# Bias addition and row minimum of a head in one VectorE instruction, early clears moved, the written-out orders redrawn

## The reference

```python
# block 1: 16 heads of 8 dims, relative-position bias, mask
energy = einsum('bhqd,bhkd->bhqk', Q, K) / sqrt(8) + bias[h, q, k]
energy = where(mask, neg, energy)
x = x + softmax(energy) @ V  (all heads) @ Wo + bo
# block 2: low-rank feed-forward with gelu, width 512
# block 3: the same attention without bias and mask
# block 4: 16 experts of width 64, each token's best 8, and a shared expert
```

## Time and profile before

| | us |
|---|---|
| median of 3 runs (lowest, highest) | 216.0 (214.54, 219.54) |
| the profiled execution | 216.93 |
| its span in the trace | 215.1 |
| PE busy in the span | 175.5 |
| DVE busy | 164.6 |
| ACT busy | 138.5 |
| POOL busy | 92.2 |

### The profile page before, as it was taken

How to read it: one execution, slowest core, us unless ns; L and a number is a source line. 1 busy time by engine, 2 the same in 40 slices (tenths; PEclk the granted TensorE clock), 3 DMA queues, 4 the chain that set the end, 5 groups by cost and what they waited for, 6 DMA issues and landing times.

```text
span 215.1 us, 4593 instructions
## 1 busy us (share of the span) xinstructions
PE 175.5 (82%) x1609; PEld 121.8 (57%) x1609; DVE 164.6 (76%) x459; ACT 138.5 (64%) x293; POOL 92.2 (43%) x109
## 2 busy tenths in 40 slices
PE   1550626999989789979759696999999999999994
PEld 0320413765556555756624493785676767788883
DVE  4269609969999999798897649599989597878643
ACT  2251404698889989999677948459389888233220
POOL 8186698699579969767123115110200011011000
PEclk9999955699999999999996978599999999999999
DMA  5352388214113650031200231200000100000000
GB/s 139 83 110 72 85 225 178 58 42 109 42 49 78 207 189 3 16 74 26 54 2 12 68 77 37 71 23 23 2 3 2 30 3 0 3 24 0 25 4 24
DMA packets 21879, 12.21 MB, mean 57 GB/s; under 512 B 3120, under 2 KB 21232, under 8 KB 21856
## 3 DMA queue, kind: packets, MB, share of 16 engines
q1 hardware_dynamic: 19776, 10.68, 19.6%
q10 hardware_dynamic: 2080, 1.24, 2.3%
HBM read 4.98 MB, written 0.54 MB: 26 GB/s over the span
## 4 chain that ended last, share of the span: by engine, by line
PE 55%; DVE 23%; ACT 5%; POOL 5%; issue 5%; SPq 2%; DMA 2%; ACTq 1%; DVEq 0%
PE bank L460 15%; PE bank L489 9%; PE bank L403 6%; PE bank L359 4%; PE bank L343 4%; DVE es L884 4%; PE bank L374 3%; DVE mx L893 3%; PE bank L439 2%; DVE q0p L1030 2%; SPq L211 2%; PE bank L476 2%; DVE x L934 2%; PE bank L429 2%; DVE ct L923 2%
## 5 line engine op out<-in xcount | busy, mean ns | idle before, releaser
L1766 POOL TENSOR_TENSOR es<-es,mx 128x512 f32<-128x512 f32 x32 | 33.6, 1065 | 8.0 <-DVE mx L889 7.8
L1744 POOL TENSOR_TENSOR rstd<-ve,half 128x2 f32<-128x2 f32 x16 | 11.1, 694 | 57.0 <-DVE ve L872 56.8
L1486 ACT ACTIVATE gth<-bank 128x256 f32<-128x256 f32 (+1 forms) x36 | 13.4, 382 | 24.6 <-PE bank L460 23.9
L403 PE MATMUL bank<-pt,va 128*32 128x128 f32 x512 | 27.3, 297 | 1.7 <-DVE es L884 0.6
L374 PE MATMUL bank<-ident,es 128*128 128x128 f32 x128 | 20.4, 291 | 4.6 <-ACT es L1426 2.9
L460 PE MATMUL bank<-xT,wg 128*128 128x256 f32 (+1 forms) x72 | 23.8, 414 | 0.0
L893 DVE TENSOR_REDUCE mx<-bank 128x4 f32<-128x512 f32 x32 | 20.5, 677 | 3.1 <-PE bank L359 3.1
L884 DVE TENSOR_TENSOR es<-bank,biasq 128x512 f32<-128x512 f32 x32 | 20.7, 679 | 2.1 <-PE bank L359 2.1
L460 PE MATMUL bank<-xT,wu 128*128 128x256 f32 (+1 forms) x72 | 21.9, 386 | 0.0
L489 PE MATMUL bank<-wd,hT 128*128 128x128 f32 x128 | 21.2, 289 | 0.0
L1426 ACT ACTIVATE es<-es 128x512 f32<-128x512 f32 x32 | 19.2, 624 | 2.8 <-POOL es L1766 2.8
(11 more groups left out here) (140 smaller groups left out, 359.4 us busy)
## 6 DMA issues: line engine op xcount, KB each, us to landing
k0st<-k0p SPq DMA_DIRECT2D x24, 64.0 KB, 2.0
k1st<-k1p SPq DMA_DIRECT2D x24, 64.0 KB, 2.0
q1st<-q1p SPq DMA_DIRECT2D x24, 64.0 KB, 2.0
q0st<-q0p SPq DMA_DIRECT2D x21, 64.0 KB, 2.0
biasq<-rel_bias_scratch SPq DMA_DIRECT2D x4, 256.0 KB, 5.2
wu<-in_wu SPq DMA_DIRECT2D x1, 544.0 KB, 3.9
wg<-in_wg SPq DMA_DIRECT2D x1, 544.0 KB, 4.9
x<-in_x SPq DMA_DIRECT2D x4, 128.0 KB, 3.7
```

What stands on the lines that cost most here:

```text
L403: ins = pe.matmul(dst[32 * s:32 * s + VW, h // 4 * SEQ:(h // 4 + 1) * SEQ], va[:, p, b, l, VCOLS * h:VCOLS * h + VW], pt[:, l, b, h], star ...
L1766: pool.tensor_tensor(es[:, b, h], es[:, b, h], mx[:, 0, p, b, h].unsqueeze(2).broadcast_to([128, 4, SEQ]), ALU.subtract).then_inc(nth(f"le ...
```

## The change

1. `add_bias` becomes four instructions, one per head of 128 columns. Each adds bias to scores and also writes the least of its row. `least` is gone, and `less_least` waits for the release of the chunk's bank, which the fourth instruction gives.
2. `first_queries_middle` makes the second bf16 part by a subtraction from the float32 values rather than by a cast of the remainder, and no longer waits for the remainder. The remainder is computed after it.
3. `value_ones` writes only the tail and the sums' columns, in two memsets; its users wait for both.
4. DVE clears both `q0` stacks first. POOL clears both `k0` stacks first, and its other clears come one or two at a time between other work, one of them (`q1`, 3) in the third quarter of the scores of block 1.
5. All lists of calls are redrawn: PE's with its banks, DVE's, ACT's, POOL's and SP's, ACT's loads of small weights among them.

The diff, cut to the new operations and to the heads of the lists:

```diff
             def values(l, p, b, c, k=None):
-                new(pe, "va_ones", 1) and pe.wait_ge(sem("va_ones"), 1)
+                new(pe, "va_ones", 2) and pe.wait_ge(sem("va_ones"), 2)
...
             front_turned(0, 1)
-            project("k0", 0, 2)
-            project("k1", 0, 3)
-            project("q0", 0, 4)
+            project("q0", 0, 2)
+            project("k0", 0, 3)
+            project("k1", 0, 4)
...
             def add_bias(p, b, c):
...
-                free(dve.tensor_tensor(es[:, b, heads(c)], src[:].rearrange("p (h k) -> p h k", h=4),
-                                       biasq[:, heads(c)], ALU.add), f"S0.{p}{b}{c}")
-
-            def least(p, b, c):
-                freed(dve, f"S0.{p}{b}{c}")
-                dve.tensor_reduce(mx[:, 0, p, b, heads(c)], es[:, b, heads(c)], AX.X, ALU.min).then_inc(nth(f"mx0{p % 2}", chunk(p // 2, b, c)), 1)
+                for s in range(4):
+                    h = heads(c).start + s
+                    ins = dve.tensor_tensor_reduce(es[:, b, h], src[:, s * SEQ:(s + 1) * SEQ], biasq[:, h], 1.0, 3.0e38,
+                                                   ALU.add, ALU.min, mx[:, 0, p, b, h:h + 1])
+                free(ins, f"S0.{p}{b}{c}")
...
+            def first_queries_middle():
+
+                freed(dve, "q0.0")
+                dve.tensor_tensor(parts["q0"][0][:, 1], whole["q0"][0][:], parts["q0"][0][:, 0], ALU.subtract).then_inc(nth("q0_first", 0), 1)
+
             def first_queries_rest():
-                freed(dve, "q0.0")
+                new(dve, "q0_first", 1) and dve.wait_ge(sem("q0_first"), 1)
                 dve.tensor_tensor(whole["q0"][0][:], whole["q0"][0][:], parts["q0"][0][:, 0], ALU.subtract).then_inc(nth("q0_first_rest", 0), 1)
 
-            def first_queries_middle():
+            def first_queries_last():
                 new(dve, "q0_first_rest", 1) and dve.wait_ge(sem("q0_first_rest"), 1)
-                dve.tensor_copy(parts["q0"][0][:, 1], whole["q0"][0][:]).then_inc(nth("q0_first", 0), 1)
...
             clear("q0", 0)
+            clear("q0", 1)
             variance(0, 0)
             mask_values()
+            shift(0, 0)
             rel_rows()
-            shift(0, 0)
             cast_ident()
             variance(0, 1)
             first_queries()
+            first_queries_middle()
             shift(0, 1)
             first_queries_rest()
-            first_queries_middle()
+            mask_bias(0)
             first_queries_last()
-            mask_bias(0)
-            clear("q0", 1)
...
+            load_wo(act)
             load_wv(act)
-            load_wo(act)
-            load_b1(act)
-            load_rows(act)
             load_bv(act)
             load_ffn(act)
+            load_rows(act)
             load_gate(act)
+            weights0(0, 0, 0)
+            load_b1(act)
+            weights0(0, 0, 1)
...
             def value_ones():
-                pool.memset(va[:], 1.0).then_inc(nth("va_ones", 0), 1)
+
+                sums = va[:, :, :, :, 0:HEADS * VCOLS].rearrange("p i b l (h v) -> p (i b l) h v", v=VCOLS)
+                pool.memset(va[:, :, :, :, HEADS * VCOLS:].rearrange("p i b l e -> p (i b l) e"), 1.0).then_inc(nth("va_ones", 0), 1)
+                pool.memset(sums[:, :, :, DK], 1.0).then_inc(nth("va_ones", 1), 1)
...
+            half_power()
             clear("k0", 0)
-            half_power()
-            value_ones()
+            clear("k0", 1)
             power(0, 0)
             power(0, 1)
             first_rest("k0", 0)
             first_rest("k1", 0)
             last_part("k0", 0)
-            clear("k0", 1)
+            last_part("k1", 0)
+            value_ones()
             clear("q1", 0)
-            clear("q1", 1)
-            last_part("k1", 0)
             first_rest("k0", 1)
             first_rest("q0", 1)
             last_part("k0", 1)
+            clear("q1", 1)
+            clear("q1", 2)
+            less_least(0, 0, 0)
+            less_least(0, 0, 1)
             last_part("q0", 1)
             clear("k1", 0)
+            less_least(0, 0, 2)
             clear("k1", 1)
-            clear("q1", 2)
-            clear("q1", 3)
-            less_least(0, 0, 0)
-            less_least(0, 0, 1)
-            power(0, 2)
-            less_least(0, 0, 2)
...
             stack(sp, "k0", 1, 1)
             load_bias(sp, 2)
+            stack(sp, "k0", 2, 1)
+            load_bias(sp, 3)
+            load_x(sp, 3)
+            load_ctx(sp, 3)
             load_x(sp, 2)
-            load_bias(sp, 3)
             load_ctx(sp, 2)
-            stack(sp, "k0", 2, 1)
```

More of the change, by code:

```diff
@@ new lines, in _ @@
+            scores0(1, 0, 2, 2, 5)
+            values(0, 0, 1, 1)
+            weights_turned(0, 1, 3, 1)
+            front_turned(2, 6)
+            values(0, 0, 1, 2)
+            scores0(1, 1, 0, 4, 2)
+            ffn_weights(2, 0)
+            values(0, 0, 1, 3)
+            scores0(1, 1, 2, 1, 5)
+            project("k0", 2, 4)
+            value_rows(2, 0, 2)
+            project("q0", 2, 6)
+            value_rows(2, 1, 3)
+            weights_turned(1, 0, 0, 1)
+            weights_turned(1, 0, 1, 4)
@@ new lines, in _ @@
+            spread(1, 1, 7)
+            spread(1, 2, 6)
+            gate_up(1, 8, 1)
+            down(1, 0, 2)
+            spread(1, 3, 3)
+            spread(1, 4, 5)
+            spread(1, 5, 7)
+            down(1, 1)
+            scores1_turned(3, 0, 0, 6, 0)
+            down(1, 2)
+            attention_out(1, 2, 3)
+            down(1, 3)
+            scores1_turned(3, 0, 2, 5, 7)
+            spread(1, 6, 4)
+            down(1, 4)
+            values(1, 3, 0, 0, 3)
+            spread(1, 7, 6)
@@ L816, in _ @@
+            gate_up(2, 5, 6)
+            combine_turned(2, 4)
+            gate_up(2, 6, 2)
+            gate_up(2, 7, 0)
+            gate_up(2, 8, 4)
+            spread(2, 0, 5)
+            spread(2, 1, 3)
+            spread(2, 2, 1)
+            spread(2, 3, 7)
+            spread(2, 4, 6)
+            down(2, 0, 5)
+            tokens_turned(3, 3, 3)
+            spread(2, 5, 1)
+            down(2, 1)
             spread(2, 6, 7)
-            spread(2, 7, 2)
-            gate_up(2, 4, 6)
@@ L1284, in _ @@
-            expert_hidden(0, 8)
-            weighted(0, 7)
-            split_max(3, 0)
-            largest(3, 1, 0)
-            largest(3, 1, 1)
+            largest(3, 1, 0)
+            split_max(3, 0)
+            largest(3, 1, 1)
+            largest(3, 1, 2)
+            context_turned(1, 2, 0)
+            output(0)
+            expert_hidden(1, 0)
+            largest(3, 1, 3)
+            router_squares(1)
+            router_best(1)
+            split_max(3, 1)
+            expert_hidden(1, 1)
@@ L1348, in _ @@
             expert_hidden(3, 2)
+            expert_hidden(3, 3)
             weighted(3, 0)
@@ L1416, in copy_values @@
             def copy_values(p, b):
-                new(act, "va_ones", 1) and act.wait_ge(sem("va_ones"), 1)
+                new(act, "va_ones", 2) and act.wait_ge(sem("va_ones"), 2)
                 src = read(act, f"v.{p}{b}")
@@ L1575, in _ @@
+            evict("k0", 3)
+            copy_values(2, 1)
             copy_turned(1, 0)
-            middle("q0", 3)
-            copy_weights(1, 1, 3)
-            copy_values(3, 1)
+            evict("q0", 3)
+            copy_values(3, 0)
             middle("k0", 3)
@@ L1647, in _ @@
-            middle("q1", 2)
             weights1(0, 1, 3)
             gelu(3, 0)
+            copy_turned(2, 2)
+            copy_max(1, 0)
             gelu(3, 1)
+            evict("q1", 2)
+            evict("k1", 3)
+            middle("q1", 2)
+            weights1(1, 0, 0)
+            middle("k1", 3)
             copy_max(1, 1)
-            weights1(1, 0, 0)
             weights1(1, 0, 1)
@@ L1764, in less_least @@
                 h = heads(c)
-                new(pool, f"mx0{p % 2}", chunk(p // 2, b, c) + 1) and pool.wait_ge(sem(f"mx0{p % 2}"), chunk(p // 2, b, c) + 1)
+                freed(pool, f"S0.{p}{b}{c}")
                 pool.tensor_tensor(es[:, b, h], es[:, b, h], mx[:, 0, p, b, h].unsqueeze(2).broadcast_to([128, 4, SEQ]),
```

969 lines of the change are left out of this document (439 added, 530 removed).

## The result

The changed kernel takes 200.7 us as median of four executions (199.75 to 203.95), beside 216.2 for the kernel before (214.54 to 219.54). Ratios use only the executions within 1.5% of the fastest of their kernel and medians use all, so the two need not agree. In two later sessions the same kernel stood at 0.9402 (0.9352 to 0.9453) and 0.9396 (0.931 to 0.9481): 13 us by these ratios, 14 to 15 by the medians (201.9 beside 216.0, 200.1 beside 214.7).

A forecast was written before the change was run, and what follows sets the result against it. No engine fills the span, so stages bound it: the start, a DVE-full stretch, an unfilled one, then PE full. 216.93 - 4.5 - 0.2 - 2 = 210.2 us, 209.3 at the median, rounded 209.5; 8-in-10 range 203.5 to 216.

The forecast's parts named there:

- signs: Trace marks of being right: first scores near 20 us, first `less_least` near 25, full-PE stretch 5 to 7 us earlier.
- The price of the subtraction: First queries on DVE: the new subtraction takes 0.41 us beside POOL's memsets, where the cast takes 4.99.
- I take 4.5 us for the whole start: Start of the kernel: removed cast stall and moved POOL clears together gain 4.5 us, with 1 and 7 as ends.
- the 0.2 for the small clears: Smaller `value_ones` and DVE's clear in its first wait: up to 3 us saved in idle times, 0.2 added.
- the cap by the bias's third part: Start: the bias's third part, issued behind pair 1's keys, limits the gain from the third chunk on to 4.1 to 4.8 us.
- I take 1.12: Fused addition on DVE: a chunk costs 1.12 us instead of 1.20, saving 2.6 us in all.
- The step from DVE's time to the end: DVE full from 55 to 75 us with PE close behind: of 2.6 us saved by the fusion, 2 arrive.
- cheap fusion: Rival, chance 0.18: the least costs nothing, DVE loses 11.5 us, some 7 arrive, giving 204.3 us.
- I count zero: Redrawn lists of all engines: they take nothing off an engine; zero gain, 4 us either way.
- Swallowed: Rival, chance 0.25: early work waits later, at 110 to 123 us; half of 6.7 us gained, redraw loses 2.3, giving 215.
- Slow fusion: Rival, chance 0.10: the fused instruction runs at half rate on DVE's full stretch, 14.4 us more, giving 224 us.

The follow-up runs named there:

- b_queries: Kernel before with only the first queries' cast replaced by a subtraction ahead of the remainder; median 210.3 us, 3.9 below the kernel before.
- b_clears: Kernel before with only the moved clears of POOL and DVE and the smaller `value_ones`, cast kept; median 208.1 us, 6.1 below the kernel before.
- a_oldclears: Changed kernel with the early part of POOL's list, clears and `value_ones`, in the old places; median 206.9 us, ratio 0.9733 to the kernel before.
- c_start: Changed kernel with two `q1` clears moved behind the first `less_least` and ACT's DMA issues behind the first two exponentials; 202.6 us, ratio 0.9419.
- c_loads: c_start with six of ACT's DMAs on SP, and `gate` and `b1` ahead of the third chunk's exponential; 200.3 us, 0.9342; again 201.2, 0.9454.
- c_bias: c_start with the bias's third and fourth loads on SP ahead of pair 1's keys; 203.2 us, ratio 0.9445.
- a_cast: Changed kernel with the old cast back in the first queries, behind the subtraction; median 201.0 us, ratio 0.9449 to the kernel before.
- b_three: Kernel before with fused addition, new subtraction, moved clears and smaller `value_ones`, other lists old; median 207.6 us, 6.5 below the kernel before.
- a_dummy: Changed kernel with a DVE memset of 336 columns behind each chunk's four fused additions; 205.2 us, ratio 0.9554 to the kernel before.
- a_dummy_front: Changed kernel with a DVE memset of 336 columns ahead of each chunk's four fused additions; 206.5 us, ratio 0.9609 to the kernel before.
- a_unfused_pairs: Changed kernel with the old addition and separate reduction, two neighbouring additions ahead of their two reductions; 206.3 us, ratio 0.9706 to the kernel before.

## Why the prediction was right or wrong

**Direction right, and most of the signs.** The stall beside the memsets is gone; the new subtraction takes 0.42 us, and no instruction of the first queries is above 1 us. The first scores stand at 19.29 us (forecast near 20), the first `less_least` at 24.10 (25), the third chunk's addition at 27.35 (28.5). Two signs were off: four fused additions take 0.85 us and not 1.1, and the first `gate_up`, my mark for the stretch in which PE is full, comes 14.1 us earlier and not 5 to 7. The price of the subtraction came from the row of L1026. A rule of the Trainium skill stood behind it ("SBUF — State Buffer", on ops that take the shared port pair). In the changed kernel POOL is idle beside the subtraction, so that trace doesn't try the rule; b_queries does, with POOL's memsets from 13.70 to 18.99, and agrees:

```profile
13.70 0.41 DVE L1027 TENSOR_TENSOR q0p<-q0f,q0p 128x256 bf16<-128x256 f32 x1
```

**The step "I take 4.5 us for the whole start": too small.** With the 0.2 for the small clears I had 4.7 us. b_clears brings 6.1 in the old lists, and a_oldclears puts the clears alone, with no stall at the cast, at 5.9 in the new; both undone together was not run there. The part that failed is the cap by the bias's third part, 4.1 to 4.8 us "from the third chunk on". In b_clears the mask is added 4.6 us earlier than before (27.60 for 32.18) and the first `attention_out` comes 6.0 earlier; in a_oldclears the mask is 0.7 later than in the changed kernel and the first `attention_out` 6.5. I had taken the third addition to set the stream, but ACT's third exponential stands behind the first chunk's `copy_values`, so the first `less_least` sets it. The attempts with c_start and c_loads show that this ends at the changed kernel: from there on, 2.8 us more at the first exponential bring nothing. That the bias is what stops them isn't shown. c_bias has the bias earlier, but also c_start's issues ahead of ACT's copy, and no run has the earlier bias without these.

The cast and the clears were steps with their own gain in my sum, and the clears alone take both: b_clears and a_cast have the cast at 0.29 us. With the clears moved the new subtraction is worth nothing, and without them it is worth the 3.9 us of b_queries.

**The step "I take 1.12": mis-sized.** It measured 0.85 us a chunk, the lower bound and the first of the rivals. I had added 0.07 us for a second output, from the row of a value load of 0.09 us, and so counted most of a row's length, where the second row here costs nothing from start to start. DVE saved 11.3 us (b_clears to b_three) and not 2.6.

**The step from DVE's time to the end: wrong in both directions.** For the 2.6 us I let 2 arrive, and for cheap fusion 7 of 11.5, on the ground that DVE was full in the earlier trace rows. In the old lists 0.5 of 11.3 us arrived. In the new lists 6.2 of 11.6 did, close to the rival's share, and 0.4 to 0.55 of the time that the clears took. A full engine in one stretch says how much it holds back there only until the next list has to wait. That DVE's freed time stood at `ct` for PE is what b_three's trace suggests.

**The step "I count zero" for the redrawn lists: the largest miss.** Alone it measured 1.8 us, not told from zero and within my 4 either way. With the fusion it is 7.5. My sum had no term for two parts that pay only together, which is 5.8 us. Along the medians of one chip the account is: clears 6.1, redraw 1.8, fusion in the new lists 6.2, 14.1 us in all (214.1 to 200.1), where the forecast had 4.7, 0 and 2.

**The rivals.** Cheap fusion had the price and, in the new lists only, nearly the gain (7 for 6.2), and gave 204.3; the result is lower for the start and the redraw. Swallowed is refuted: the gain grows from 8.7 to 14.1 us between the first `attention_out` and the first `gate_up`. Slow fusion is refuted by the 284 ns rows.

**What stays open.** In the new lists the unfused form costs 6.2 us. The clears of a_dummy cost 3.3 and those of a_dummy_front 4.5, for 7.9 and 8.2 us of DVE's busy time. Scaled to the 11.6 of the unfused form that is an estimate of 4.8 and 6.4 us, so DVE's time and the turn can cover the 6.2, within wide intervals. POOL's longer wait for the least is a candidate beside them (6.1 us for nine waits in a_unfused_pairs from 34 to 96 us), but no run isolated it. Which of PE's, DVE's and ACT's redrawn lists makes the fusion pay was not tried, so why the two pay together is argued and not shown. Nor was it measured what part of the gain comes by the higher clock of PE from 34 to 44 us.

## What to carry to other kernels

Price an edit that frees an engine by what the other engines' orders would do with the time: where every queue is in a fixed order, freed time can bring almost nothing until the orders are drawn for it (here 0.5 against 6.2 us), so a cheaper instruction and a redraw should be judged together and not as a sum. Price small back-to-back instructions from start to start, not by their row's length, and bound a secondary row by zero below. Before reading a wait in one execution as the work of the order, compare the granted clock of that stretch. Before giving two edits a gain each, ask whether either of them alone removes the same stall.

## What the runs showed of the hardware

The accumulator's read-out takes 81 ns in its row and nothing from start to start. A reduction right behind the addition that it depends on starts 0.71 us after it, at its end, where the next independent instruction starts 0.60 us on (73.43 to 74.03). Dependence costs some 0.1 us a pair.

GpSimd and VectorE hinder each other in more than the cast. VectorE's four mask additions, with both inputs in SBUF, take 0.68, 1.15, 1.20 and 1.34 us in the changed kernel (mean 1094 ns), where one of the same shape took 0.69 in the earlier trace rows; the three long ones begin beside a subtraction of POOL. In a_oldclears two of them lie beside memsets and take 0.69 each. The last part of the first queries takes 0.89 us beside a subtraction of POOL, and 0.43 beside a memset in b_queries. The addition of 0.68 ran beside a subtraction too, from 12.03, but there it was POOL that lost time. POOL's of 128 x 256 takes 1.23 us, against the 0.67 of `k0`'s last part, as large, in b_clears:

```profile
12.01 1.23 POOL L1725 TENSOR_TENSOR k0f<-k0f,k0p 128x256 f32<-128x256 f32 x1 [3.83 <-ACT k0f L1378]
```

The subtraction that ran in the earlier trace rows beside a memset took 0.41 us, and three in b_queries 0.41 to 0.43. So of two instructions with both inputs in SBUF, one on each engine, one or both lose time, and a memset slows a cast but not a subtraction, as far as these few rows go.
